# A four-layer graph network on one core: the third sort inside the first eight attention blocks, linear scores as table columns, operands in PSUM

## The chip, the cores and the metric

The kernel runs on one core of a Trainium2 chip. The time is device microseconds (us) of one execution. In the text, PE is TensorE (matmul), DVE is VectorE, ACT is ScalarE, POOL is GpSimd and SP is SyncE, whose queue only starts transfers here. SBUF is the on-chip memory of 128 partitions; PSUM is the smaller one that PE writes its sums into, which DVE and ACT can read and write too.

## The reference

3125 nodes with 64 features, 100000 edges sorted by destination, and four layers in a row, each on the normalised and rectified features, each added to its input. The layer that the change is about is the first:

```python
def _L0_gnn_ref(node_attr, edge_index, Wl, Wr, att, W1, b1, W2, b2):   # N = 3125, H = 4, DH = 16
    ngl = (node_attr @ Wl.T).reshape(N, H, DH)
    ngr = (node_attr @ Wr.T).reshape(N, H, DH)
    idx = jnp.concatenate([edge_index, edge_index[:, ::-1]], axis=0)      # every edge both ways
    src, dst = (idx[:, 0], idx[:, 1])
    gl = ngl[src]
    gr = ngr[dst]
    score = (att * jax.nn.leaky_relu(gl + gr, SLOPE)).sum(-1)             # SLOPE = 0.2
    m = jax.ops.segment_max(score, src, num_segments=N)
    ex = jnp.exp(score - m[src])
    denom = jax.ops.segment_sum(ex, src, num_segments=N)
    alpha = ex / (denom[src] + 1e-16)
    out = jax.ops.segment_sum(gr * alpha[:, :, None], src, num_segments=N)
    ...
```

The second layer (twice) and the third need sums of neighbours' rows over the 100000 edges, and the second a sum of the edges' own 64 attributes by destination. The fourth is an attention with eight heads over 31250 edges' worth of blocks of its own.

## The kernel before

The program is written by engine: one instruction stream each for SP, POOL, ACT, DVE and PE, ordered by hand and tied by semaphores. A `wait_ge` stops the engine that executes it, and all that stands behind it on that engine.

**Preparation (0 to 1324 us of the trace).** POOL scatters the edge attributes to records in DRAM (`scatter_recs`, L695: 98 groups of eight indirect DMAs of 128 rows each), then the 50 chunks of own rows (L715). Beside it DVE counts degrees with one-hot comparisons (`ones_of`, L1049: 336 bf16 comparisons of `iotab` with the edges' numbers, both in SBUF; PE multiplies them), and sorts three times with a bitonic network on 128 x 1024 numbers (`ordered`: 87 full comparison steps of a minimum and a maximum, L1203 and L1206; 66 partial ones of four instructions, L1212; 14 turns, in which PE transposes the block and DVE copies it back from PSUM, L1231 and L1233; 8 sign changes, L1220; 175 stages in all). The first two sorts order the edges by source and by destination for the attention; the third one (`KL`/`SBL` in the tile `oh`) orders them by cell of the adjacency matrix. Only the matrix units (below) need the third.

**The first attention (1324 to 3757 us).** 54 blocks of 128 partitions x 32 edge slots. For block g:

- POOL (`gather`, L738) waits until DVE has used the ring slot of block g - 4 (`taken0`, semaphore `av`), waits in `hold` (L688, a tiny addition on `pdum`) for the block's index list `jst`, and issues 32 indirect DMAs of 128 rows of 64 numbers from `tab[0]` into `G0`, a ring of four blocks. Before block 3 stands `gather_keys`: a hold for the third sort's result in DRAM, and nine indirect DMAs (L728) of windows of it.
- SP (`load_block`, L563) loads `jst` of block g + 3 once DVE has begun block g + 1 or so (`after(sp, S["aow"], b.g - 2)`), and stores the finished rows.
- DVE (`block0`): own rows (L1387), sum with the gathered rows (L1437, two halves of 1024), leaky slope (L1440, two), times `att` (L1442, two; `attb_ps` lies in PSUM), sum over 16 columns (L1444), then eleven short operations of the running maximum (L1395 to L1408). Then, beside the attention: matrix units (`matrix_ones`, L1414: one bf16 comparison of 2048 numbers of `iotab` with `SD`, both in SBUF, for each) and record groups (`rec_ones`, L1423). Then weights times rows (L1453, two; the weights are columns of `V0` in SBUF, which ACT fills), a sum over each row's four slots (L1460, from `V0` into `RS0`, both SBUF), and the carried scan (L1465 to L1467, `DX0` and `RS0` in SBUF).
- PE (`beside0`) multiplies each matrix unit (L1902) and each record group (L1910); ACT (`weights0`) takes the exponentials and casts and stores the units.

There are 272 units, `UAT`: five for each of the first 48 blocks, and `UL`: 6, 5, 5, 6, 5, 5 in the last six. Record groups: two a block, in the last six 4, 5, 4, 5, 4, 4. The first 48 blocks run as a loop of four, the last six are written out. Between the third sort and block 0, DVE and PE make the unit tables `SD` out of the nine windows (L1344 to L1355).

**After it** come the fix-up of rows cut by partitions, the neighbour sums of layers two and three, the second attention (same `gather` and L738, rows of 72 numbers) and the end.

## Time and profile before

| | us |
|---|---|
| median of 3 runs | 6147.66 |
| lowest, highest | 6140.43, 6149.96 |
| the profiled execution's own time | 6139.35 |
| its span | 6137.6 |

By stage, from the busy time of each engine in windows (us from the span's start):

| stage | length | DVE busy | POOL busy | PE busy |
|---|---|---|---|---|
| attribute scatter, degrees, two sorts, part of the third (109 to 1242) | 1133.0 | 946.6 | 901.0 | 385.6 |
| own rows (1242 to 1324) | 82.0 | 69.6 | 59.9 | 11.8 |
| blocks 0 to 2 are gathered (1324 to 1457) | 133.0 | 97.4 | 104.3 | 13.8 |
| key windows, unit tables (1457 to 1498) | 41.0 | 21.9 | 9.1 | 4.0 |
| blocks 3 to 53 (1498 to 3714) | 2216.0 | 1651.7 | 1725.2 | 695.4 |
| last block on DVE (3714 to 3757) | 43.0 | 35.3 | 0.7 | 19.1 |
| everything behind the first attention (3757 to 6137.6) | 2380.6 | | | |

### The profile page before, as it was taken

To read this page: it belongs to the slowest core of one execution; us is meant where nothing else is said; L and a number is where in the kernel's file an instruction comes from. 1 tells how busy PE (TensorE), PEld (TensorE's weight loads), DVE (VectorE), ACT (ScalarE), POOL (GpSimd) and SP (SyncE) were. 2 spreads that over 40 slices of the span, in tenths; PEclk is the share of its full clock that TensorE was granted. 3 is DMA by queue.
4 is the path that set the end of the run, shared out by engine and by line. 5 is a ranking of instruction groups with operands and counts; after the bars stand their busy time and mean duration, and the time that the engine had idled before them with its cause. 6 is when DMAs were issued, how large, how long until landed. Compare 5 with 4: busy or idle time off the path is not lost.

```text
span 6137.6 us, 56339 instructions
## 1 busy us (share of the span) xinstructions
PE 2661.9 (43%) x13332; PEld 1809.3 (29%) x13333; DVE 4092.7 (67%) x6865; ACT 1253.9 (20%) x4370; POOL 3783.2 (62%) x3760
## 2 busy tenths in 40 slices
PE   1785101011332322222222342677674577777746
PEld 0661101011322222222222242546453232332315
DVE  9778888886986776767676774232322576676655
ACT  0000000000111111111111110000000677777741
POOL 2777777776777777777777774000002777777730
PEclk6555555555555555555555555767685788888876
DMA  6221121211222222222222231435261222332230
GB/s 229 53 54 51 48 56 48 73 29 50 77 79 61 72 61 71 63 70 64 69 64 68 66 85 39 144 104 179 69 205 22 58 83 77 87 86 77 84 98 7
DMA packets 388365, 472.44 MB, mean 77 GB/s; under 512 B 212478, under 2 KB 248384, under 8 KB 381041
## 3 DMA queue, kind: packets, MB, share of 16 engines
q1 hardware_dynamic: 132624, 279.73, 13.8%
q0 software_dynamic: 114832, 129.82, 9.7%
q10 hardware_dynamic: 140752, 61.28, 3.5%
q14 instruction: 116, 0.94, 0.0%
q8 instruction: 41, 0.67, 0.0%
HBM read 291.34 MB, written 179.19 MB: 77 GB/s over the span
## 4 chain that ended last, share of the span: by engine, by line
POOL 58%; issue 21%; PE 9%; DMA 6%; DVE 5%; ACT 0%; POOLq 0%; DVEq 0%; ACTq 0%; SPq 0%
POOL arena L738 44%; POOL rec_dram L695 11%; PE acc L1959 4%; DMA oh<-mt_dram 2%; PE acc L1780 2%; DMA V<-in_edge_attr_dram 2%; DMA rec_dram<-V,rowst 1%; PE acc L1782 1%; PE acc L1943 1%; POOL own_dram L715 1%; POOL pdum L688 1%; POOL arena L765 1%; DVE arena L1579 1%; PE pt L1770 0%; POOL own_dram L769 0%
## 5 line engine op out<-in xcount | busy, mean ns | idle before, releaser
L738 POOL DMA_INDIRECT arena<-tab_dram,jst x2592 | 2685.8, 1036 | 778.3 <-issue 777.8
L695 POOL DMA_INDIRECT rec_dram<-V,rowst x784 | 866.1, 1105 | 229.9 <-issue 217.8
L688 POOL TENSOR_TENSOR pdum<-pdum 128x1 f32<-128x1 f32 x197 | 58.5, 297 | 1138.3 <-DVE arena L1607 864.6
L1902 PE MATMUL pw<-OHX 128*128 128x128 bf16 x1632 | 210.3, 310 | 1120.8 <-DVE OHX L1414 1120.8
L1902 PEld LDWEIGHTS pw<-OHX 128*128 128x128 bf16 x1632 | 156.9, 140 | 1172.3 <-DVE OHX L1414 859.7
L1910 PE MATMUL acc<-arena,oh 128*128 128x64 f32 x1952 | 427.1, 420 | 20.9 <-DVE oh L1423 20.7
L1910 PEld LDWEIGHTS acc<-arena,oh 128*128 128x128 f32 x1952 | 417.2, 330 | 34.9 <-issue 34.9
L900 ACT ACTIVATE arena<-arena,ew 128x64 f32<-128x64 f32 x1728 | 417.8, 333 | 33.3 <-PE acc L1983 33.3
L1437 DVE TENSOR_TENSOR arena<-arena,pt 128x1024 f32<-128x1024 f32 x108 | 131.8, 1221 | 431.7 <-DMA arena<-tab_dram,jst 429.4
L900 ACT ACTIVATE OHX<-arena,ew 128x64 f32<-128x64 f32 x1728 | 417.7, 333 | 2.5
L1983 PE MATMUL acc<-OHX,ident 128*128 128x512 f32 x432 | 253.7, 753 | 371.0 <-ACT OHX L900 371.0
L1855 PE MATMUL acc<-ident,oh 128*128 128x128 f32 x336 | 82.7, 427 | 752.3 <-DVE vdum L1224 752.3
L1212 DVE TENSOR_TENSOR oh<-oh 128x256 f32<-128x256 f32 x792 | 341.6, 431 | 37.8
L1855 PEld LDWEIGHTS acc<-ident,oh 128*128 128x128 f32 x336 | 65.9, 223 | 770.2 <-DVE vdum L1224 770.2
L855 ACT ACTIVATE arena<-dc 128x476 f32<-128x476 f32 x54 | 57.5, 1065 | 1143.3 <-DVE dc L1405 1143.3
L1959 PE MATMUL acc<-V,oh 128*128 x1440 | 234.7, 321 | 106.4 <-DVE arena L1579 86.5
L1579 DVE TENSOR_TENSOR arena<-arena,acc 128x192 f32 x360 | 127.6, 355 | 214.2 <-PE acc L1959 207.7
L1414 DVE TENSOR_TENSOR OHX<-iotab,OHX 128x2048 bf16<-128x2048 bf16 x204 | 249.7, 1224 | 28.0 <-DVE OHX L1414 15.6
L1983 PEld LDWEIGHTS acc<-OHX,ident 128*128 128x128 f32 x432 | 103.8, 248 | 520.1 <-issue 520.1
L825 ACT COPY V<-arena 128x8 f32 (+1 forms) x98 | 20.1, 205 | 1157.6 <-DMA rec_dram<-V,rowst 1080.5
L1902 PE MATMUL pw<-oh 128*128 128x128 bf16 x544 | 70.2, 310 | 386.2 <-DVE oh L1414 386.2
L1049 DVE TENSOR_TENSOR OHX<-iotab,arena 128x364 bf16<-128x364 bf16 x336 | 180.3, 536 | 64.5 <-DVE OHX L1049 17.9
(523 smaller groups left out, 6463.2 us busy)
## 6 DMA issues: line engine op xcount, KB each, us to landing
oh<-mt_dram SPq DMA_DIRECT2D x90, 512.0 KB, 3.6
arena<-tab_dram,jst POOLq DMA_INDIRECT x2592, 2.5
arena<-rec_dram SPq DMA_DIRECT2D x122, 288.0 KB, 3.6
mt_dram<-oh ACTq DMA_DIRECT2D x272, 128.0 KB, 1.7
oh<-mt_dram SPq DMA_DIRECT2D x75, 416.0 KB, 3.9
oh<-mt_dram SPq DMA_DIRECT2D x75, 384.0 KB, 4.0
rows_dram<-V SPq DMA_DIRECT2D x27, 1056.0 KB, 4.0
rows_dram<-arena SPq DMA_DIRECT2D x27, 1056.0 KB, 4.3
```

Source lines behind the costliest of these rows:

```text
L695: gp.indirect_dma_start(rec[:, :], bass.IndirectOffsetOnAxis(ap=rowst[:, q, k:k + 1], axis=0), recst[:, q, k, :], None).then_inc(S[f"scat{ ...
L738: gp.indirect_dma_start(hd.G[:, a.r, j, :], None, table[:, :], row_of(jst[:, a.r, j:j + 1])).then_inc(S[f"{x}g{a.r}"], 16)
L900: last = A.activation(V3r[vslot[f]][:, (k * H3 + h) * D:(k * H3 + h + 1) * D], G3[:, a.r, t, 0:D], ACT.Copy, scale=ew[:, a.q, t * H3 + h:t ...
L1049: V.tensor_tensor(paired(o[:, a:a + n]), iota_pairs(n, wide, EP), values[:, k, :].unsqueeze(2).to_broadcast([EP, n, wide // 2, 2]), ALU.is ...
L1212: V.tensor_tensor(o[r], a[r], b[r], op).then_inc(S["v"], 1)
L1414: V.tensor_tensor(paired(mones[c.slot].rearrange("p o t n -> p (o t) n")), iota_pairs(2 * GT, P), SD[:, bass.ds(c.u * (4 * GT), 4 * GT)].r ...
L1579: V.tensor_tensor(o, o, group_sum(g), ALU.add).then_inc(S["cadd"], 1)
L1855: last = nc.tensor.transpose(acc[:, (first + b) * P:(first + b + 1) * P], src[:, b * P:(b + 1) * P], ident[:])
L1902: last = nc.tensor.matmul(unit_bank(c.slot)[:, k // 2 * P:(k // 2 + 1) * P], mones[c.slot][:, 0, k, :], mones[c.slot][:, 1, k, :], start=k ...
L1910: last = nc.tensor.matmul(o, roh[:, c.q, k, :], RG[:, c.r, k, 0:D], start=False, stop=True, skip_group_check=True)
L1959: last = nc.tensor.matmul(group_sum(g), mring[:, slot, g * 4 + k, :], hsp[:, bass.ds(rows[g * 4 + k] * (3 * D), 3 * D)], start=k == 0, sto ...
L1983: last = nc.tensor.matmul(row_bank(2 * f + k // RK), ident[:], V3r[vslot[f]][:, k * 512:(k + 1) * 512], start=k % RK == 0, stop=k % RK == ...
```

## The change

Five things change together.

1. **Third sort in the blocks.** The list of 175 stages is cut: the first 104 run where the whole sort stood, the other 71 in eight parts inside DVE's blocks 0 to 7, behind the scores. The sort's two buffers move from `oh` to `OHX` (`SB3`), its transposes on PE from `acc` to `pw`. SP stores the keys behind block 7 (`store_keys`), POOL gathers the windows before block 12, and the unit tables are made in DVE's block 13 (`units_ready`), through `pw` in three parts.
2. **Units later.** Blocks 0 to 13 have no matrix units; blocks 14 to 53 have 272 x (g - 14) / 40 rounded down, so six or seven each. The blocks are written out on ACT, DVE and PE in place of the loop of four.
3. **Linear scores in the table.** leaky(z) is 0.2 z + 0.8 max(z, 0). The 0.2 part of the gathered row, times `att`, summed by head, is computed once for each node (`LIN`) and stored as four more columns of `tab[0]`, so a gathered row has 68 numbers. The own row's linear part is the same for all edges of a softmax and is left out. In the block one instruction does max and multiply.
4. **Weights, sums and compared numbers in PSUM.** ACT writes the weights a second time into PSUM (`wexp_ps`); the sums over slots go to `sums_ps` in two halves, so do the scans; `iotab` is copied to `pairs_ps`, which all one-hot comparisons read, those of the degree count too.
5. **Waits that go with it**: `tb` counts three tables, `ax` four activations a block, DVE waits for all weights' loads before `LIN`.

```diff
+SORTED_IN, SORT_FRONT = 8, 104
+UNITS_AT, KEYS_AT = SORTED_IN + 6, SORTED_IN + 4
...
-        KI = ohf_[:, 0:MT].bitcast(I)
-        KI2 = OHXf[:, 6400:6400 + MT // 2].bitcast(I)
+        SB3 = [OHXf[:, k * SWL:(k + 1) * SWL] for k in range(2)]
+        KI, KI2 = [OHXf[:, k * 1024:(k + 1) * 1024].bitcast(I) for k in range(2)]
...
-        iota_ps, attb_ps = pt[:, 512:512 + P], pt[:, 512 + P:512 + P + D]
+        pairs_ps, attb_ps = pt[:, 512:512 + P // 2], pt[:, 512 + P // 2:512 + P // 2 + D]
         own_ps = pt[:, 0:RB * D].rearrange("p (f d) -> p f d", d=D)
+        wexp_ps = pt[:, 0:TB * H0].rearrange("p (t h o) -> p t h o", h=H0, o=1)
+        half_x = (D + H0) // 2
+        sums_ps = [pt[:, k:k + half_x * RB] for k in (TB * H0, 1024 - half_x * RB)]
...
+        def unit_at(g):
+
+            return max(g - UNITS_AT, 0) * NU // (NB0 - UNITS_AT)
...
+        def sort_part(g):
+
+            rest = len(edge_sort) - SORT_FRONT
+            at_ = [0 if h < 0 else SORT_FRONT + rest * min(h, SORTED_IN) // SORTED_IN for h in (g, g + 1)]
+            return edge_sort[at_[0]:at_[1]]
...
-                quads(gp, n, rows)
+                if hd is heads0:
+                    quads(gp, n, rows, 0, KEYS_AT // 4)
+                    held[0] += KEYS_AT
+                    gather_keys()
+                    held[0] -= KEYS_AT
+                    quads(gp, n, rows, KEYS_AT // 4)
+                else:
+                    quads(gp, n, rows)
...
+                A.activation(wexp_ps, ew[:, a.q, 0:TB * H0].rearrange("p (t h o) -> p t h o", h=H0, o=1), ACT.Exp).then_inc(S["ax"], 1)
...
-                return iotab[0:parts, 0:wide].rearrange("p (n e) -> p n e", e=2).unsqueeze(1).to_broadcast([parts, tiles, wide // 2, 2])
+                return pairs_ps.bitcast(BF)[0:parts, 0:wide].rearrange("p (n e) -> p n e", e=2).unsqueeze(1).to_broadcast([parts, tiles, wide // 2, 2])
...
-            V.tensor_copy(GR, acc_n).then_inc(S["tsrc"], 1)
+            v.wait_ge(S["wts"], 16 * 29)
+            link(V.tensor_copy(GR, acc_n))
+            link(V.tensor_tensor(nbr_r[:], GR, attb[:].unsqueeze(1).to_broadcast([P, NC, D]), ALU.mult))
+            link(V.tensor_reduce(LIN, nbr_r[:].rearrange("p c (h e) -> p c h e", h=H0), AX, ALU.add))
+            V.tensor_scalar(LIN, LIN, SLOPE, None, ALU.mult).then_inc(S["tsrc"], 1)
...
+                    for hf in range(2):
+                        wv = work[:, hf * 1024:(hf + 1) * 1024].rearrange("p (t d) -> p t d", d=D)
+                        st(V.scalar_tensor_tensor(wv, wv, 0.0, attb_ps.unsqueeze(1).to_broadcast([P, TB // 2, D]), ALU.max, ALU.mult))
                     st(V.tensor_reduce(sc[:, 0:TB * H0], work.rearrange("p (x e) -> p x e", e=D // H0), AX, ALU.add))
+                    by_head = sc[:, 0:TB * H0].rearrange("p (t h) -> p t h", h=H0)
+                    st(V.tensor_tensor(by_head, by_head, Ga[:, :, D:D + H0], ALU.add))
                 scores(heads0, a, st, summed)
+                if a.g < SORTED_IN:
+                    sort_more(a)
+                if a.g == UNITS_AT - 1:
+                    units_ready()
...
+                for k, part in enumerate(sums_ps):
+                    ins = V.tensor_reduce(part.rearrange("p (x f) -> p f x", f=RB), V0[:, :, 2 * k:2 * k + 2].rearrange("p (f k) h e -> p f (h e) k", k=RK), AX, ALU.add)
```

**POOL, from the own rows to the first gathers**, before and then changed: `own_dram` is the own rows' scatter, `ps` two single gathers, `arena<-tab_dram,jst` a block of 32, `OHX<-keys_dram` the key windows, `pdum` the holds.

```order
L715 DMA own_dram<-arena,rst_u 61696x64 x50
L688 TENSOR_TENSOR pdum<-pdum 128x1 x2
L719 DMA ps<-tabl_dram,nfi 128x64 x2
...
L688 TENSOR_TENSOR pdum<-pdum 128x1
L738 DMA arena<-tab_dram,jst 128x64 x32
L688 TENSOR_TENSOR pdum<-pdum 128x1 x3
L728 DMA OHX<-keys_dram,arena 128x256 x8
L728 DMA OHX<-keys_dram,arena 64x256
L688 TENSOR_TENSOR pdum<-pdum 128x1
L738 DMA arena<-tab_dram,jst 128x64 x32
```

```order
L729 TENSOR_TENSOR pdum<-pdum 128x1
L779 DMA arena<-tab_dram,jst 128x68 x32
L385 REGISTER_ALU
L385 COMPARE_AND_BRANCH
L729 TENSOR_TENSOR pdum<-pdum 128x1 x3
L769 DMA OHX<-keys_dram,arena 128x256 x8
L769 DMA OHX<-keys_dram,arena 64x256
```

Before, the key windows stand behind the third block's gathers; now they stand behind the loop that ends with the twelfth, and a gathered row has 68 numbers.

**DVE, block 0 of the first attention from the gathered rows on**, before and then changed (`arena` holds the gathered rows, `work`, `DX0` and `RS0`; `pt` is PSUM; `OHX` and `oh` hold the one-hot tables; the eleven short operations of the maximum stand where the first row of "..." is).

```order
L1437 TENSOR_TENSOR arena<-arena,pt 128x1024 x2
L1440 SCALAR_TENSOR_TENSOR arena<-arena 128x1024 x2
L1442 TENSOR_TENSOR arena<-arena,pt 128x1024 x2
L1444 TENSOR_REDUCE sc<-arena 128x128
...
L1414 TENSOR_TENSOR OHX<-iotab,OHX 128x2048 x3
L1414 TENSOR_TENSOR oh<-iotab,OHX 128x2048
L1414 TENSOR_TENSOR OHX<-iotab,OHX 128x2048
L1423 TENSOR_TENSOR oh<-pt,arena 128x1024 x2
L1453 TENSOR_TENSOR V<-arena,V 128x64x16 x2
L1460 TENSOR_REDUCE arena<-V 128x8x68
L1465 TENSOR_TENSOR V<-V,dc 128x68
L1466 TENSOR_TENSOR arena<-arena,V 128x68
```

```order
L1495 TENSOR_TENSOR arena<-arena,pt 128x1024 x2
L1499 SCALAR_TENSOR_TENSOR arena<-arena,pt 128x1024 x2
L1500 TENSOR_REDUCE sc<-arena 128x128
L1502 TENSOR_TENSOR sc<-sc,arena 128x128
...
L1261 TENSOR_TENSOR OHX<-OHX 128x32x2x4 x4
...
L1483 TENSOR_TENSOR oh<-pt,arena 128x1024 x2
L1515 TENSOR_TENSOR V<-arena,pt 128x64x16 x2
L1523 TENSOR_REDUCE pt<-V 128x8x34 x2
L1531 TENSOR_TENSOR V<-V,dc 128x68
L1534 TENSOR_TENSOR pt<-pt,V 128x34 x2
L1537 SCALAR_TENSOR_TENSOR V<-arena,pt 128x272 x2
```

The five comparisons of block 0 have become eight stages of the sort (from L1261 on); multiply, reduce and scan have one operand in `pt` where both lay in SBUF.

## Rows read from the trace of the kernel before

**Rows 1.** The page, chain that ended last, by line: share of the span.

```profile
POOL arena L738 44%; POOL rec_dram L695 11%; PE acc L1959 4%; DMA oh<-mt_dram 2%; PE acc L1780 2%; DMA V<-in_edge_attr_dram 2%; DMA rec_dram<-V,rowst 1%; PE acc L1782 1%; PE acc L1943 1%; POOL own_dram L715 1%; POOL pdum L688 1%; POOL arena L765 1%; DVE arena L1579 1%; PE pt L1770 0%; POOL own_dram L769 0%
```

**Rows 2.** POOL's timeline: start us, duration us, what, [idle before <-releaser].

```profile
1324.04 1.08 POOL L738 DMA_INDIRECT arena<-tab_dram,jst  x1 [0.16 <-issue]
...
1456.87 0.74 POOL L688 TENSOR_TENSOR pdum<-pdum 128x1 f32<-128x1 f32 x3
...
1497.68 0.19 POOL L688 TENSOR_TENSOR pdum<-pdum 128x1 f32<-128x1 f32 x1 [28.89 <-DMA jst<-meta_dram]
...
3712.89 0.94 POOL L738 DMA_INDIRECT arena<-tab_dram,jst  x1 [0.30 <-issue]
```

**Rows 3.** POOL's groups, 1498 to 3715 us: count, busy us, mean ns, idle.

```profile
L738 POOL DMA_INDIRECT arena<-tab_dram,jst x1632 | 1714.2, 1050 | 489.9 <-issue 489.6
```

**Rows 4.** Timeline of POOL and of DVE, around 1506 us.

```profile
1506.47 1.92 POOL L738 DMA_INDIRECT arena<-tab_dram,jst  x1 [0.30 <-issue]
...
1506.35 3.74 DVE L1414 TENSOR_TENSOR OHX<-iotab,OHX 128x2048 bf16<-128x2048 bf16 x3
```

**Rows 5.** Timeline of POOL and of DVE, 1562 to 1568 us.

```profile
1563.64 0.94 POOL L738 DMA_INDIRECT arena<-tab_dram,jst  x1 [0.30 <-issue]
...
1566.13 1.17 POOL L738 DMA_INDIRECT arena<-tab_dram,jst  x1 [0.30 <-issue]
...
1562.75 2.48 DVE L1437 TENSOR_TENSOR arena<-arena,pt 128x1024 f32<-128x1024 f32 x2
1565.26 2.48 DVE L1440 SCALAR_TENSOR_TENSOR arena<-arena 128x1024 f32<-128x1024 f32 x2
```

**Rows 6.** Timeline of POOL and of DVE, while the third sort runs.

```profile
1395.76 1.15 POOL L738 DMA_INDIRECT arena<-tab_dram,jst  x1 [0.30 <-issue]
...
1395.39 0.69 DVE L1203 TENSOR_TENSOR oh<-oh 128x512 f32<-128x512 f32 x1
```

**Rows 7.** POOL's groups, 180 to 440 us, then 440 to 447; DVE's by form.

```profile
L695 POOL DMA_INDIRECT rec_dram<-V,rowst x180 | 198.7, 1104 | 54.2 <-issue 51.2 <-DMA V<-in_edge_attr_dram 3.0
...
L695 POOL DMA_INDIRECT rec_dram<-V,rowst x6 | 5.8, 965 | 1.8 <-issue 1.8
...
L1049 DVE TENSOR_TENSOR OHX<-iotab,arena 128x896 bf16<-128x896 bf16 x224 | 140.7, 628 | 32.7 <-DVE OHX L1049 9.4
```

**Rows 8.** DVE's groups by form, 1490 to 3757 us.

```profile
L1414 DVE TENSOR_TENSOR OHX<-iotab,OHX 128x2048 bf16<-128x2048 bf16 x204 | 249.7, 1224 | 28.0 <-DVE OHX L1414 15.6 <-DVE oh L1414 6.9 <-PE pw L1902 4.5
L1460 DVE TENSOR_REDUCE arena<-V 128x544 f32<-128x2176 f32 x54 | 209.2, 3874 | 1.9
...
L1440 DVE SCALAR_TENSOR_TENSOR arena<-arena 128x1024 f32<-128x1024 f32 x108 | 132.7, 1229 | 3.7
...
L1437 DVE TENSOR_TENSOR arena<-arena,pt 128x1024 f32<-128x1024 f32 x108 | 131.8, 1221 | 431.7 <-DMA arena<-tab_dram,jst 429.4
...
L1467 DVE TENSOR_TENSOR_SCAN V<-arena 128x544 f32<-128x544 f32 x54 | 69.8, 1292 | 1.9
...
L1395 DVE TENSOR_TENSOR sc<-sc,jst 128x128 f32<-128x128 f32 x54 | 17.2, 318 | 1.9
```

**Rows 9.** DVE's timeline: blocks 21, 49 and 53 begin.

```profile
2327.11 2.48 DVE L1437 TENSOR_TENSOR arena<-arena,pt 128x1024 f32<-128x1024 f32 x2 [10.85 <-DMA arena<-tab_dram,jst]
...
3548.47 2.48 DVE L1437 TENSOR_TENSOR arena<-arena,pt 128x1024 f32<-128x1024 f32 x2 [5.00 <-DMA arena<-tab_dram,jst]
...
3716.24 2.47 DVE L1437 TENSOR_TENSOR arena<-arena,pt 128x1024 f32<-128x1024 f32 x2 [1.79 <-DMA arena<-tab_dram,jst]
```

**Rows 10.** DVE's groups, whole span: a 2048-number cast out of PSUM.

```profile
L1349 DVE CAST oh<-acc 128x2048 int32<-128x2048 f32 x1 | 2.3, 2293 | 4.1 <-PE pt L1888 4.1
```

**Rows 11.** Line L738, both attentions: duration ns min/median/max, first and last start us.

```profile
L738 POOL DMA_INDIRECT arena<-tab_dram,jst x2592: 940/944/2000, 1324.0 to 5870.2; - x200
```

**Rows 12.** DVE's timeline: begin and end of the third sort.

```profile
1136.07 86.55 DVE L1212 TENSOR_TENSOR oh<-oh 128x256 f32<-128x256 f32 x180
...
1436.84 0.06 DVE L1340 MEMSET vdum<- 1x1 f32 x1
```

More of the change, by code:

```diff
@@ L387, in quads, with spans @@
                     body(Group(n // 4, t))
-        def spans(eng, n, ahead, step):
+        def spans(eng, n, ahead, step, cut=4, between=None):
             def at(i, t):
@@ L395, in spans @@
                 at(0, t)
-            with eng.Fori(1, whole) as i:
-                for t in range(4):
-                    at(i, t)
+            for i, e in ((1, cut // 4), (cut // 4, whole)):
+                if i == cut // 4 and between:
+                    between()
+                if i + 1 == e:
+                    for t in range(4):
+                        at(i, t)
+                elif i < e:
+                    with eng.Fori(i, e) as turn:
+                        for t in range(4):
+                            at(turn, t)
             for t in range(4 * whole, n):
@@ L531, in _ @@
             table(1, GL, tabl)
-            table(2, GR, tab[0])
+            table(2, GR, tab[0][:, 0:D])
+            table(2, LIN, tab[0][:, D:D + H0])
             sp.wait_ge(S["pre"], 3)
```

269 lines of the change are left out of this document (146 added, 123 removed).

## The prediction, made before the changed kernel ran

> **What bounds the kernel now.** I read the chain that ended last first: 44% of the span is one line, POOL's row gathers of the two attentions [rows 1]. So the question for each stage is whether POOL ever waits. In POOL's timeline over the first attention the reader is to see that it begins at 1324.04, gathers blocks 0 to 2 until 1456.87, does the nine key windows, stands 28.89 us, and from 1497.68 to 3713.83 never stands again [rows 2]. The releaser named is block 3's index list, but SP could not issue it before DVE began block 0, and DVE began late since it still had to finish the third sort and the unit tables. DVE in turn waits 10.85 us before block 21, of a period of 2370.81 - 2327.11 = 43.7 us (the next start is the next block's): it has 32.9 us of work in a block [rows 9]. The first attention is POOL's.
>
> Then I asked what one gather costs. The median is 0.944 us with a minimum of 0.940, for rows of 64 and of 72 numbers together [rows 11], but the mean of the 1632 gathers of blocks 3 to 53 is 1.050, with 0.30 between two [rows 3]. The difference, 1632 x 0.106 = 173 us, is what DVE does to POOL. Seen one by one: a gather that begins 0.12 us after a comparison with both inputs in SBUF takes 1.92, and ends 0.8 us behind the end of that comparison, the first of three in 3.74 us [rows 4]. One that begins while DVE adds an SBUF and a PSUM operand takes 0.94; one that begins 0.4 us before the first of two slope operations (both inputs `work`) ends takes 1.17, which is that end plus 0.8 again [rows 5]. Reading all gathers of the stretch against DVE's rows that way, those that begin outside an operation with two SBUF inputs never exceed 0.96. While the sort runs, gathers keep step with two of its 0.69 us operations and take 1.15, so 1.45 a piece with the gap instead of 1.244 [rows 6].
>
> **A rule against this.** The Trainium skill, "SBUF — State Buffer", section "Who interferes with whom", tells of a probe in which `tensor_copy` held up GpSimd's DMAs and `tensor_tensor` did not. Rows 4 to 6 differ: here it does, and the rows decide. By the rule the PSUM operands would give POOL nothing, which is rival 2.
>
> **The change, part by part**, in the trace's own time (span 6137.6, execution 6139.35).
>
> *Degree count.* Its comparisons read `pairs_ps` instead of `iotab`. In 180 to 440 us, 180 scatters take 1.104 us; when the comparisons have ended, six take 0.965 [rows 7]. POOL scatters without a pause, so all behind moves forward: 180 x 0.139 = **-25**. From below 0, if only half is port and DMA staging takes the rest. `LIN` adds some 6 us to DVE (three passes over 1600 numbers), which DVE has: it ends the second sort long before POOL needs it. The wait for the weights' loads is moved to where they have long landed.
>
> *The idle time before block 3.* The whole sort took 1436.84 - 1136.07 = 300.8 us [rows 12]. Its 66 partial steps cost 86.55/45 = 1.92 each, the 87 full ones 2 x 0.69 + 0.07 = 1.45, so 14 turns and 8 sign changes share 48. The front, 52 partial, 40 full, seven turns, five signs, is 100 + 58 + 24 = 182 us and ends near 1136 + 6 + 182 = 1324; the rest is 119, or 14.9 a block. DVE is then ready before block 0's rows have landed (1299 + 43), SP's queue reaches the index list of block 3 at once, and the wait of 28.89 is gone: **-29**. The key windows (12 us) only move, and the unit tables, which fitted into that wait, go into DVE's block 13, which has no units. What queues behind that wait on DVE is only its own block: POOL is a ring of four ahead.
>
> *Blocks.* POOL now needs 132.8 for blocks 0 to 2 and 2216.2 for the other 51 [rows 2], together 2349.0. A clean block is 32 x (0.944 + 0.30) + 0.5 for hold and wait = 40.3. Comparisons, slope, weights times rows and scan lose their second SBUF input; what keeps two is short (0.2 to 0.37 us each, as L1395 [rows 8]), say 0.1 a block: 40.4. In the first eight blocks 14.9 us of sort cover ten gathers that lose 0.2 each: 42.4. While the front still runs beside block 0, 3.3 more. Sum 8 x 42.4 + 46 x 40.4 + 3.3 = 2200.9: **-148**.
>
> A row of 68 numbers lies between widths that share one median [rows 11], so it costs nothing.
>
> *What hides DVE's work.* Two of 1.229 go, one of 0.32 comes, the split sums and scans add some 0.3: -1.9 [rows 8]. In the first eight blocks also five comparisons of 1.26 go and 14.9 of sort come: 32.9 - 1.9 - 6.3 + 14.9 = 39.6, under POOL's 42.4. Blocks 14 to 47 have 6.8 units: 32.9 - 1.9 + 2.3 = 33.3, under 40.4. Not seen before are sums and scans into and out of PSUM. The two sums cost at least 2.4, by 1024 numbers in 1.221, at most 2 x 3.87; I take 4.0, near the one they replace. The scans lie between 1.3 and 2.6; I take 1.4. With both at their worst the block is 38.3, still covered in the middle. ACT's additional exponential of 128 numbers is hidden by the sort, the units or the two record groups.
>
> *The end.* The last six blocks have 26 record groups that alternate with PE, and DVE needs about 40.6, 42.8, 39.7, 44.1 and 39.4 for blocks 48 to 52 (ends of [rows 9]: only 1.79 us is left before block 53). That was hidden by 43.4. With -1.9, and one or two more units each, they are 40.0, 42.2, 40.3, 43.5 and 40.0 against 40.4: DVE falls 4.4 behind, and block 53 is 0.6 longer: **+5**, or +35 with sums and scans at their worst.
>
> Sum: -25 - 29 - 148 + 5 = -197, so 5942 for such an execution. The median of the runs was 8.3 above the profiled one: **5951 us**.
>
> **Rivals.**
> 1. *PSUM takes the double rate away.* The comparison of 2048 bf16 numbers takes 1.224 [rows 8], twice the rate of f32, where 2048 out of PSUM take 2.293 [rows 10]. No row shows bf16 out of PSUM. If it goes at the single rate, the 336 of the degree count take 224 x 0.47 + 112 x 0.19 = 126 us more, DVE begins block 0 near 1450, POOL has ended block 2 at 1432 and waits 23, with 5 more under the sort; the 41 units of the last six blocks add 41 x 1.07 = 44. Together 5951 + 72 = **6023**. The Trainium skill, "VectorE: DVE Perf Modes", has this rule in "The perf-mode tier table" (`tensor_tensor` with any PSUM operand 1x), while its section "Why PSUM operands drop a tier" leaves the packed 2x mode open. Against it: f32 with one PSUM operand costs what two SBUF ones cost (1.221 and 1.229 [rows 8]).
> 2. *POOL gets nothing from PSUM operands.* Then only the wait goes, and the sort slows eight blocks: 8 x 44.8 + 46 x 43.4 = 2355, +6, with -29 and +1: 6117 + 8 = **6126**. Against it stand rows 4 and 5.
> 3. *DVE becomes the bound: slower than before.* From 7.1 us a block above my 33.3 it sets the pace of blocks 14 to 53, and from some 12 it eats all. Comparisons at the single rate (7.3), sums at 7.7 (+3.7) and scans at 2.6 (+1.2) would do it: 40 x (45.5 - 40.4) = 204, with 28 at the start and 12 more at the end **6195**. It needs every PSUM operand dear at once, which the f32 rows speak against.
>
> **How the numbers follow.** My forecast has 0.78, rival 1 0.11, rival 2 0.08, rival 3 0.03. The forecast's own range is 5920 (DVE's sums at the low bound, blocks at 40.3, more scatters freed) to 6000 (no gain in the degree count, or the worst end). With rival 1 it reaches to 6040; rivals 2 and 3 are left out, and the edges of the others. Within 0.2% is about 12 us, what a measurement of this kernel can tell from no change: faster 0.96, same 0.01, slower 0.03.
>
> **What would show it.** In the changed profile: scatters of 180 to 440 us at 0.97; block 3's hold with no wait; the group of the first attention's gathers at a mean near 0.95, about 1.0 in blocks 0 to 7; DVE's comparison at 1.22 (2.29 is rival 1); a wait of some 7 us on DVE for rows in the middle blocks and none in the last six; POOL's last gather near 3512, DVE's last block near 3557. A mean of 1.05 would be rival 2. Wrong would be also a new wait of POOL on `av` (DVE more than three blocks late), or gathers of 68 numbers at more than 0.95 on their own.

## The result, and the profile of the changed kernel

The changed kernel takes **5926.45 us** (median of four runs, 5924.3 to 5928.3) against 6147.95 before; the ratio is 0.9642, with a 95% interval of 0.9625 to 0.9658. The forecast was 5951, in a range of 5920 to 6040. The profiled execution of the changed kernel took 5926.62 with a span of 5923.7, so 213.9 us of span are gone, where the sum said 197.

In the page of the changed kernel the row gathers of the two attentions, now on line L779, still head the chain that ended last, with 35% of the span in place of 44% [rows 1]:

```profile
POOL arena L779 35%; POOL rec_dram L736 11%; PE acc L2039 4%; DMA oh<-mt_dram 2%; DVE OHX L1473 2%; PE acc L1854 2%; PE acc L1856 1%; PE acc L2023 1%; POOL own_dram L756 1%; DMA V<-in_edge_attr_dram 1%; DMA rec_dram<-V,rowst 1%; PE acc L1990 1%; DVE oh L1483 1%; DVE arena L1495 1%; DVE V L1515 1%
```

POOL's groups of the changed kernel, first from 180 to 440 us (the degree count's stretch, as [rows 7]), then from 1296 to 3489 us (all 54 blocks of the first attention, as [rows 3]). Columns: count | busy us, mean ns | idle before, releaser:

```profile
L736 POOL DMA_INDIRECT rec_dram<-V,rowst x200 | 195.1, 976 | 60.1 <-issue 60.1
...
L779 POOL DMA_INDIRECT arena<-tab_dram,jst x1728 | 1650.7, 955 | 518.5 <-issue 515.5 <-DVE V L1515 3.0
```

The first row: 200 scatters fit where 180 did, 0.976 us each instead of 1.104. The second: a gather takes 0.955 on the mean instead of 1.050, and nearly all idle time is the 0.30 between two. POOL's and DVE's timelines of the changed kernel show the ends of the stages (start, duration, what, [idle before <-releaser]), as [rows 2, 9]:

```profile
1296.12 0.96 POOL L779 DMA_INDIRECT arena<-tab_dram,jst  x1 [0.35 <-issue]
...
1420.43 0.21 POOL L729 TENSOR_TENSOR pdum<-pdum 128x1 f32<-128x1 f32 x1
...
3487.79 0.94 POOL L779 DMA_INDIRECT arena<-tab_dram,jst  x1 [0.30 <-issue]
...
3532.95 1.47 DVE L1537 TENSOR_TENSOR_SCAN V<-arena,pt 128x272 f32<-128x272 f32 x2
```

The gathers begin at 1296.12 instead of 1324.04. The hold of block 3 (the addition on `pdum` at 1420.43) waits for nothing; before it waited 28.89. The last gather ends at 3488.73 instead of 3713.83, and DVE's last scan at 3534.42, 45.7 behind it; before these were 39.1 (3752.90 behind 3713.83). DVE's groups by form, 1640 to 3536 us, answer to [rows 8]; below them, the scan that ended before's last block:

```profile
L1473 DVE TENSOR_TENSOR OHX<-pt,OHX 128x2048 bf16<-128x2048 bf16 x204 | 249.5, 1223 | 5.9
L1523 DVE TENSOR_REDUCE pt<-V 128x272 f32<-128x1088 f32 x94 | 191.4, 2037 | 3.2
...
L1499 DVE SCALAR_TENSOR_TENSOR arena<-arena,pt 128x1024 f32<-128x1024 f32 x92 | 112.3, 1220 | 3.1
...
L1537 DVE TENSOR_TENSOR_SCAN V<-arena,pt 128x272 f32<-128x272 f32 x94 | 67.7, 720 | 3.2
```

```profile
3751.61 1.29 DVE L1467 TENSOR_TENSOR_SCAN V<-arena 128x544 f32<-128x544 f32 x1
```

A bf16 comparison with one input in PSUM still takes 1.223, so rival 1 is out. The Trainium skill, "VectorE: DVE Perf Modes", has it at the single rate in the section "The perf-mode tier table" and leaves the packed rate open in "Why PSUM operands drop a tier"; this row shows the double rate. The two sums take 4.07 (4.0 assumed), the two scans 1.44 (1.4).

**The books.** From the start of the span to the first gather: -27.9. The idle time before block 3: -28.9. The blocks: before 2349.0 (the prediction's own count), now 3488.73 - 1296.12 = 2192.6, less 12.0 for the key windows in block 12, is 2180.6: -168.4. From POOL's last gather to DVE's last scan: +6.6. What follows: +4.6, nearly all in the neighbour sums, which the change doesn't touch: POOL waits there for DVE 864.6 us in the profile of before, 869.3 in the changed kernel's and 866.3 to 871.9 in those of parts 1, 3 and 4 below, whatever was changed, so before's profile had a short one. With 0.1 for the key windows the sum is -213.9.

A gather is called caught below when it lasts clearly longer than its own 0.944 us, and its excess is what it lasts over 0.944. Added up over the 1728 gathers of the first attention, the excess was 186 us before and is 20 now, nearly all of it in blocks 0 to 8 and in block 14.

### The profile page after: what moved, and what is told of

Its sections match the earlier page's. It is cut to its first block, busy times and chain, and to the rows that moved or that the text cites. A ratio compares the mean times of both kernels' runs of the same rounds, so it can differ in the third digit from the quotient of the medians.

```text
span 5923.7 us, 53534 instructions
## 1 busy us (share of the span) xinstructions
PE 2662.1 (45%) x13332; PEld 1808.8 (31%) x13333; DVE 4000.1 (68%) x6981; ACT 1264.8 (21%) x4424; POOL 3582.9 (60%) x3760
## 4 chain that ended last, share of the span: by engine, by line
POOL 50%; issue 20%; DVE 13%; PE 11%; DMA 5%; ACT 0%; POOLq 0%; DVEq 0%; SPq 0%; ACTq 0%
POOL arena L779 35%; POOL rec_dram L736 11%; PE acc L2039 4%; DMA oh<-mt_dram 2%; DVE OHX L1473 2%; PE acc L1854 2%; PE acc L1856 1%; PE acc L2023 1%; POOL own_dram L756 1%; DMA V<-in_edge_attr_dram 1%; DMA rec_dram<-V,rowst 1%; PE acc L1990 1%; DVE oh L1483 1%; DVE arena L1495 1%; DVE V L1515 1%
## 5 line engine op out<-in xcount | busy, mean ns | idle before, releaser
L779 POOL DMA_INDIRECT arena<-tab_dram,jst x2592 | 2519.3, 972 | 778.1 <-issue 775.0
L736 POOL DMA_INDIRECT rec_dram<-V,rowst x784 | 837.5, 1068 | 231.6 <-issue 224.0
L729 POOL TENSOR_TENSOR pdum<-pdum 128x1 f32<-128x1 f32 x197 | 53.1, 270 | 1122.5 <-DVE arena L1681 869.3
L1929 PE MATMUL acc<-ident,oh 128*128 128x128 f32 x224 | 55.1, 428 | 487.7 <-DVE vdum L1273 487.7
L1473 DVE TENSOR_TENSOR OHX<-pt,OHX 128x2048 bf16<-128x2048 bf16 x204 | 249.5, 1223 | 5.9
L1261 DVE TENSOR_TENSOR oh<-oh 128x256 f32<-128x256 f32 x528 | 227.6, 431 | 24.6
L1523 DVE TENSOR_REDUCE pt<-V 128x272 f32<-128x1088 f32 x108 | 219.9, 2037 | 3.7
L1096 DVE TENSOR_TENSOR OHX<-pt,arena 128x364 bf16<-128x364 bf16 x336 | 178.6, 532 | 64.2 <-PE pt L1905 18.5
L2023 PE MATMUL acc<-V,oh 128*128 128x192 bf16 x1875 | 174.3, 251 | 88.7 <-DMA oh<-mt_dram 52.4
```

What stands on the lines that cost most here:

```text
L736: gp.indirect_dma_start(rec[:, :], bass.IndirectOffsetOnAxis(ap=rowst[:, q, k:k + 1], axis=0), recst[:, q, k, :], None).then_inc(S[f"scat{ ...
L779: gp.indirect_dma_start(hd.G[:, a.r, j, :], None, table[:, :], row_of(jst[:, a.r, j:j + 1])).then_inc(S[f"{x}g{a.r}"], 16)
L1261: V.tensor_tensor(o[r], a[r], b[r], op).then_inc(S["v"], 1)
L1473: V.tensor_tensor(paired(mones[c.slot].rearrange("p o t n -> p (o t) n")), iota_pairs(2 * GT, P), SD[:, bass.ds(c.u * (4 * GT), 4 * GT)].r ...
L1523: ins = V.tensor_reduce(part.rearrange("p (x f) -> p f x", f=RB), V0[:, :, 2 * k:2 * k + 2].rearrange("p (f k) h e -> p f (h e) k", k=RK), ...
L2023: last = nc.tensor.matmul(group_sum(a.t // 2), mring[:, a.t % 4, k, :], hsp[:, j * (3 * D):(j + 1) * (3 * D)], start=j == 0, stop=j == NC ...
```

## Experiments

Each kernel's runs stand beside runs of the kernel before on the same chip. Differences from the changed kernel are against its median of 5926.45. With the chip of part 2 left out, before's medians were 6142.1 to 6148.0, so a difference between kernels of two chips is good to some 6 us.

**1. One part undone at a time.** Four kernels on one chip (before: 6142.1 there).

The first, `u1_compare_sbuf`:

```diff
                 V.tensor_tensor(paired(mones[c.slot].rearrange("p o t n -> p (o t) n")),
-                                iota_pairs(2 * GT, P),
+                                iota_sbuf(2 * GT, P),
...
-                V.tensor_tensor(roh[:, c.q], pairs_ps.bitcast(BF).unsqueeze(1).to_broadcast([P, GT, P]),
+                V.tensor_tensor(roh[:, c.q], iotab[:].unsqueeze(1).to_broadcast([P, GT, P]),
```

> The changed kernel with one part undone: the comparisons of the first attention's matrix units and record groups read their row of numbers from SBUF again. In the kernel before, the excess over 0.944 us of the gathers that began in such a comparison adds up to 78 us over 51 blocks, 1.5 a block. Theory A (each comparison costs what it cost there): 40 blocks with units and 54 with record groups give +60 to +80 us, gathers' mean about 1.00. Theory B (a train of comparisons brings the gathers into step with it, 1.26 us each instead of 1.244, so that only the first of a train costs much): +12 to +20. Rival 2 of the prediction (the operand's place doesn't matter to POOL): within 0.2% of the changed kernel.

Measured: 5962.0 us, **+35.6**, between the two theories and nearer to B. The edit undoes more than the change did: in the kernel before only the matrix units' comparisons read SBUF alone; those of the record groups read PSUM already (`oh<-pt,arena`, L1423). Here, and in `u4_blocks_sbuf` and `u6_all_sbuf` below, these read SBUF too, and the gathers that they catch have an excess of 12 to 13 us, some 7 of it in blocks 49 to 53. So what the change moved is worth some 23 of the 35.6. The next, `u2_degree_sbuf`, undoes the degree count's operand alone:

```diff
-                    V.tensor_tensor(paired(o[:, a:a + n]), iota_pairs(n, wide, EP),
+                    V.tensor_tensor(paired(o[:, a:a + n]), iota_sbuf(n, wide, EP),
```

> The changed kernel with the degree count's comparisons reading from SBUF again, nothing else. My theory: the scatters of 180 to 440 us go back from 0.976 to about 1.10 us each and all behind them starts 28 us later (1324 instead of 1296 for the first gather): +28 in the total. If something else had moved the start forward, no change.

Measured: 5956.8, **+30.4**. POOL's group of 180 to 440 us is back where before's was [rows 7], or a little above (1.125 us each, 1.104 before):

```profile
L736 POOL DMA_INDIRECT rec_dram<-V,rowst x179 | 201.4, 1125 | 52.2 <-issue 50.4 <-DMA V<-in_edge_attr_dram 1.8
```

`u3_sort_front` does the whole third sort ahead of the blocks:

```diff
-SORTED_IN, SORT_FRONT = 8, 104
+SORTED_IN, SORT_FRONT = 8, 175
```

> The changed kernel with all 175 stages of the third sort ahead of block 0, none in the first eight blocks. DVE then begins block 0 near 1443 us instead of 1340. My theory: the gathers of blocks 0 to 2 keep step with the sort (1.45 us each with the gap, 46.4 a block instead of 41.6: +14), POOL stands about 15 us before block 3, and blocks 3 to 8 run at 40.1 instead of 41.7 (-10): +20 us. If carrying the sort into the blocks had brought nothing: no change.

Measured: 5944.1, **+17.7**. In POOL's timeline the gathers of blocks 0 to 2 keep step with the sort, and the hold of block 3 waits again:

```profile
1343.47 1.13 POOL L779 DMA_INDIRECT arena<-tab_dram,jst  x1 [0.30 <-issue]
...
1429.95 1.14 POOL L779 DMA_INDIRECT arena<-tab_dram,jst  x1 [0.30 <-issue]
...
1447.92 0.20 POOL L729 TENSOR_TENSOR pdum<-pdum 128x1 f32<-128x1 f32 x1 [16.82 <-DMA jst<-meta_dram]
```

`u4_blocks_sbuf` has the edit of the first, and:

```diff
-            link(V.tensor_scalar(attb_ps, attb[:], 1.0 - SLOPE, None, ALU.mult))
+            link(V.tensor_scalar(attb_sb[:], attb[:], 1.0 - SLOPE, None, ALU.mult))
...
-                        st(V.scalar_tensor_tensor(wv, wv, 0.0, attb_ps.unsqueeze(1).to_broadcast([P, TB // 2, D]), ALU.max, ALU.mult))
+                        st(V.scalar_tensor_tensor(wv, wv, 0.0, attb_sb[:].unsqueeze(1).to_broadcast([P, TB // 2, D]), ALU.max, ALU.mult))
...
-                                          wexp_ps[:, ts].to_broadcast([P, TB // 2, H0, D // H0]), ALU.mult)
+                                          V0[:, ts, :, D // H0:].to_broadcast([P, TB // 2, H0, D // H0]), ALU.mult)
```

> As the first, and also the weights and the attention vector of the slope operation come from SBUF again; only the sums, the scans and the degree count keep PSUM. By theory A the shares in the kernel before add up: 78 for the comparisons, 34 for the slope operation, 14 for the weights, 1.05 as the gathers' mean: +110 to +125. By theory B the second and third add little: +18 to +40.

Measured: 5970.1, **+43.6**: with the weights and the attention vector it is 8 us more than with the comparisons alone. Theory A (110 to 125) is refuted, and theory B (18 to 40) is passed by 4. The three parts undone give 30.4 + 17.7 + 43.6 = 92 of the 221.5 us between the two medians, and some 12 of them are the record groups', so more than half of the gain doesn't come back when they are undone.

**2. Four more kernels, of which only one told something.** On the chip that ran them every kernel was some 1800 us longer (before 7952.2), and in the profiles the engines stood at moments for 10 to 20 us, DVE in the degree count for up to 113 us, in front of an instruction, released by what the profile calls "remote". POOL waited there for index lists that depend on DVE's progress, 848 us in `b1_compare_psum`, where the kernel before has 36, so DVE set the pace, and the four are not compared with the others.

`b1_compare_psum`, made from the kernel before:

```diff
-                V.tensor_tensor(paired(mones[c.slot].rearrange("p o t n -> p (o t) n")), iota_pairs(2 * GT, P),
+                V.tensor_tensor(paired(mones[c.slot].rearrange("p o t n -> p (o t) n")),
+                                pairs_ps.bitcast(BF).rearrange("p (n e) -> p n e", e=2).unsqueeze(1).to_broadcast([P, 2 * GT, P // 2, 2]),
```

> The kernel before with one part of the change alone: the comparisons of the matrix units in the first attention read their row of numbers from PSUM. In the trace of before such a block has one gather of 1.92 us and four of 1.07 to 1.09 under the five comparisons, 1.5 us over 0.944 together. Theory A (what is undone is gained): 51 x 1.5 = -77 us. Theory B (a gather caught by one operation shifts all behind it, so others are caught instead): -25 to -60. If the place of the operand doesn't matter: no change.

Measured: 8003.4 against 7952.2, ratio 1.0068 (1.0046 to 1.0091): inconclusive, and not repeated.

`b3_straight`, made from the kernel before:

```diff
-            quads(eng, NB0, body, 0, LAST // 4)
-            for t in range(LAST, NB0):
+            for t in range(NB0):
                 body(Group(t // 4, t % 4))
```

> The kernel before with another part alone: the blocks of the first attention written out on PE, ACT and DVE instead of a loop over four, no operand moved. In before DVE stands 0.15 us between two comparisons of the loop and their pitch is 1.38 us; in the changed kernel without the loop it is 1.26, next to the 1.24 of the gathers. Theory B: the four later gathers under the comparisons take 0.95 instead of 1.08, 47 blocks x 0.5 = -25 us. Rival: the loop only costs DVE, which has slack, so no change.

Measured: 7970.0, ratio 1.0024 (1.0010 to 1.0038): inconclusive, repeated below.

`u5_all_sbuf` has the edits of `u4_blocks_sbuf`, and:

```diff
-        sums_ps = [pt[:, k:k + half_x * RB] for k in (TB * H0, 1024 - half_x * RB)]
+        sums_ps = [arena[:, 12800:12800 + half_x * RB], arena2[:, 6112:6112 + half_x * RB]]
```

> The changed kernel with comparisons, weights, attention vector, sums and scans of the first attention all in SBUF again (u4_blocks_sbuf plus sums and scans; the degree count keeps PSUM). The excess of gathers that began in the scan of before was 46 us over 51 blocks. Theory A: +48 over u4_blocks_sbuf. Theory B (two scans of 0.70 us, less to be caught by, and the phase is as it falls): +10 to +35 over it, so 5980 to 6005.

Measured: 7909.9, ratio 0.9937 (0.9913 to 0.9962): inconclusive, repeated below.

`p1_kinds` is the kernel of part 3 with one operation of each kind and another list of kinds.

> The changed kernel with one more DVE operation at the start of each of blocks 16 to 47, where DVE waits for rows anyway (its output is overwritten, nothing is left out): four blocks for each kind. Kinds in order: tensor_tensor f32 with both inputs in SBUF; the same with one in PSUM; tensor_reduce f32; copy f32; tensor_scalar f32; copy bf16; tensor_tensor bf16 with both in SBUF; tensor_scalar bf16, all from SBUF. Theory: only the first and the seventh make a gather that starts in them last until their end plus 0.8 us (up to 3.1 us for one of 2.3); under all others gathers take 0.94. Rival: what matters is an operation's speed, so the fast copies hold gathers too and the first, at 1 number a cycle, doesn't. The total: within 0.3% of the changed kernel.

Measured: 7865.0. The total says nothing, but a gather can be read against the operation in which it begins on any chip. Under the first kind, gathers that began 0.84 and 1.25 us into 2.3 took 2.26 and 1.89; under the second and third all took 0.94. But a gather that began 0.33 into the fifth kind, an f32 `tensor_scalar` with one input, took 1.71, which is its end plus 0.8, and the two copies and the bf16 `tensor_scalar` caught gathers too (1.38 to 1.60). My theory of two SBUF inputs was too narrow.

**3. Which operations hold a gather.**

```diff
+            def probe(kind):
...
+                times, op = ((2, lambda: V.tensor_tensor(f32, f32, att_s, ALU.mult)),
+                             (2, lambda: V.tensor_tensor(f32, f32, att_p, ALU.mult)),
+                             (2, lambda: V.tensor_copy(f32, att_p)),
+                             (3, lambda: V.tensor_copy(f32, att_s)),
+                             (3, lambda: V.tensor_scalar(f32, f32, 0.5, None, ALU.mult)),
+                             (3, lambda: V.tensor_copy(b16, row)),
+                             (2, lambda: V.tensor_reduce(sc[:, 0:TB * H0], work.rearrange("p (x e) -> p x e", e=D // H0), AX, ALU.max)),
+                             (3, lambda: V.tensor_scalar(b16, row, 0.5, None, ALU.mult)))[kind]
...
+                if H == H0 and 16 <= a.g < 48:
+                    probe((a.g - 16) // 4)
                 v.wait_ge(S[f"{x}g{a.r}"], (a.turn + 1) * 16 * TB)
```

> p1_kinds again with operations in pairs or threes, so that more gathers begin in each kind. p1_kinds showed that my theory of two SBUF inputs is too narrow: a tensor_scalar of 2048 f32 in 1.23 us held a gather as well. New theory: what holds POOL is an operation with two inputs in SBUF at any rate, or one with one SBUF input at the fast rate (2048 f32 or 4096 bf16 in 1.23 us); one with a PSUM input, and a reduction, never do. Kinds in order: tensor_tensor f32 both SBUF; tensor_tensor f32 one PSUM; copy f32 out of PSUM; copy f32 SBUF; tensor_scalar f32 SBUF; copy bf16 SBUF; tensor_reduce f32; tensor_scalar bf16 SBUF. Expected: gathers begun in the first, fourth, fifth, sixth and eighth end 0.8 us behind the operation in which they began; in the second, third and seventh all take 0.94. Total within 0.5% of the changed kernel.

Measured: 5964.8 (before 6143.8 beside it). POOL's gathers of four blocks for each kind, in the order of the expectation (the stretches 1966 to 2135, 2136 to 2295, 2296 to 2455, 2456 to 2623, 2625 to 2792, 2793 to 2960, 2962 to 3120 and 3122 to 3289 us):

```profile
L779 POOL DMA_INDIRECT arena<-tab_dram,jst x128 | 130.3, 1018 | 38.4 <-issue 37.5 <-DVE V L1535 0.9
...
L779 POOL DMA_INDIRECT arena<-tab_dram,jst x128 | 120.8, 944 | 38.4 <-issue 38.1 <-DVE V L1535 0.3
...
L779 POOL DMA_INDIRECT arena<-tab_dram,jst x128 | 120.8, 944 | 38.4 <-issue 37.8 <-DVE V L1535 0.6
...
L779 POOL DMA_INDIRECT arena<-tab_dram,jst x128 | 129.1, 1009 | 38.4 <-issue 37.8 <-DVE V L1535 0.6
...
L779 POOL DMA_INDIRECT arena<-tab_dram,jst x127 | 128.1, 1008 | 38.2 <-issue 37.6 <-DVE V L1535 0.6
...
L779 POOL DMA_INDIRECT arena<-tab_dram,jst x128 | 129.4, 1011 | 38.4 <-issue 38.4
...
L779 POOL DMA_INDIRECT arena<-tab_dram,jst x128 | 120.9, 944 | 38.4 <-issue 38.4
...
L779 POOL DMA_INDIRECT arena<-tab_dram,jst x128 | 129.3, 1010 | 38.4 <-issue 38.4
```

Five kinds raise the mean, as expected: both inputs in SBUF, and every one-input operation from SBUF at the fast rate. Three don't: one input in PSUM, a copy out of PSUM, a reduction. The fifth kind in the timelines of DVE and POOL:

```profile
2658.15 3.75 DVE L1440 TENSOR_SCALAR arena<-arena 128x2048 f32<-128x2048 f32 x3
...
2657.76 1.73 POOL L779 DMA_INDIRECT arena<-tab_dram,jst  x1 [0.30 <-issue]
2659.80 2.22 POOL L779 DMA_INDIRECT arena<-tab_dram,jst  x1 [0.30 <-issue]
```

The first of these gathers began 0.39 us ahead of the three operations and was held all the same, to 0.11 behind the end of the first (1.23 us); the second to 0.12 behind the end of the third. That I had not expected: where another fast operation follows at once, the gather does not end 0.8 us behind the operation in which it began, as I had written, but 0.12 behind the next. It still ends 0.82 behind where none follows: in the fifth kind's fourth block one gather began in the last of the three and took 1.66. In the four fast kinds every gather that began up to 0.48 ahead was caught, and those that began 0.77 ahead, and in `p1_kinds` 0.53 ahead, took their 0.94. Under the two-input operation those that began 0.37 to 0.39 ahead took 0.94. The Trainium skill, "SBUF — State Buffer", section "Who interferes with whom", says that copies and `tensor_scalar` at the two-port rates block GpSimd, that reductions don't, and, as an inference, that `tensor_tensor` doesn't hold descriptor generation. The rows agree with the first two and contradict the third.

**4. The rest of the gain, and a version that goes on.** Three kernels on one chip (before: 6143.6).

> The same kernel as b3_straight, on a chip on which the kernel before runs at its usual time: the kernel before with the blocks of the first attention written out, no operand moved. Theory B: the gaps of 0.15 us between two comparisons go, gathers keep step with them at 0.95 instead of 1.08: -25 us. Rival: the loop costs DVE alone, which has slack: no change.

The edit is that of b3_straight. Measured: 6107.6, **-35.9** (ratio 0.9940, 0.9924 to 0.9957), more than the 25 expected. The loop cost POOL, not DVE alone: 33 of it are less excess in the first attention (186 to 153 us), by the profiles. DVE's and POOL's timelines in one block of the middle:

```profile
2530.55 2.48 DVE L1439 SCALAR_TENSOR_TENSOR arena<-arena 128x1024 f32<-128x1024 f32 x2
...
2540.28 1.22 DVE L1413 TENSOR_TENSOR OHX<-iotab,OHX 128x2048 bf16<-128x2048 bf16 x1
2541.53 1.22 DVE L1413 TENSOR_TENSOR oh<-iotab,OHX 128x2048 bf16<-128x2048 bf16 x1
2542.78 3.74 DVE L1413 TENSOR_TENSOR OHX<-iotab,OHX 128x2048 bf16<-128x2048 bf16 x3
...
2556.15 1.29 DVE L1466 TENSOR_TENSOR_SCAN V<-arena 128x544 f32<-128x544 f32 x1
...
2530.71 1.88 POOL L737 DMA_INDIRECT arena<-tab_dram,jst  x1 [0.30 <-issue]
...
2540.39 1.91 POOL L737 DMA_INDIRECT arena<-tab_dram,jst  x1 [0.30 <-issue]
2542.61 0.95 POOL L737 DMA_INDIRECT arena<-tab_dram,jst  x1 [0.30 <-issue]
2543.87 0.95 POOL L737 DMA_INDIRECT arena<-tab_dram,jst  x1 [0.30 <-issue]
...
2556.43 1.77 POOL L737 DMA_INDIRECT arena<-tab_dram,jst  x1 [0.30 <-issue]
```

The comparisons follow at 1.26 us. The first gather among them begins 0.11 behind the start of the first comparison and is caught until 0.8 behind its end. Each later one begins 0.13 to 0.14 before the end of a comparison, and 0.82 behind that end is also where its own 0.95 ends: it runs at 0.95 + 0.31 = 1.26, in step with them, so a train of operations costs once. In the loop of before DVE stood 0.15 between two comparisons, their pitch was 1.38, and in most blocks each later gather among them took 1.07 to 1.09, waiting for the same 0.82 behind an end that came 0.13 later. What is left in this block is one catch each in the slope operation, the first comparison and the scan: 0.94 + 0.97 + 0.83 = 2.7.

> The same kernel as u5_all_sbuf, on a chip on which the kernel before runs at its usual time: comparisons, weights, attention vector, sums and scans of the first attention in SBUF again. Theory A (each scan costs what it cost in before, 46 us together): 6018. Theory B (what an operation costs depends on where the gathers fall against it, so the sum of the shares of before is not to be had back): 5980 to 6005.

The edit is that of u5_all_sbuf. Measured: 5971.2, **+44.7**, which is `u4_blocks_sbuf` again (5970.1): sums and scans in PSUM are worth about 1 us, no more than the two chips differ by, and even theory B's 10 was too much. The same kinds of operands stand in SBUF as in `b4_straight`, and those of the record groups as well, yet a block of the middle loses half as much:

```profile
2557.51 2.48 DVE L1504 SCALAR_TENSOR_TENSOR arena<-arena,attb_sb 128x1024 f32<-128x1024 f32 x2
...
2565.07 1.22 DVE L1478 TENSOR_TENSOR OHX<-iotab,OHX 128x2048 bf16<-128x2048 bf16 x1
...
2582.62 1.48 DVE L1542 TENSOR_TENSOR_SCAN V<-arena 128x272 f32<-128x272 f32 x2
...
2557.63 1.92 POOL L780 DMA_INDIRECT arena<-tab_dram,jst  x1 [0.30 <-issue]
...
2564.87 1.11 POOL L780 DMA_INDIRECT arena<-tab_dram,jst  x1 [0.30 <-issue]
2566.28 0.95 POOL L780 DMA_INDIRECT arena<-tab_dram,jst  x1 [0.30 <-issue]
...
2583.78 1.08 POOL L780 DMA_INDIRECT arena<-tab_dram,jst  x1 [0.30 <-issue]
```

The slope operation still catches a gather (1.92). The gather at the comparisons began in the short subtraction ahead of them and lost 0.17 instead of 0.97; the next began 0.04 ahead of a comparison and took 0.95. The one at the scan lost 0.14 instead of 0.83. In both kernels DVE starts a block when the rows of a gather land, so its operations stand at nearly fixed offsets against the gathers; here, with one wide multiplication gone, one short addition in and the scan halved, the offsets are better.

How sharp an offset is, the slope operation of this one kernel shows. Of the 31 blocks 17 to 47, 20 are like the one above and take 41.4 us; in the other 11 the slope operation catches none, and they take 40.2. In `b4_straight` most take 42.9. Such a block of the other sort, DVE and POOL:

```profile
2517.44 2.48 DVE L1504 SCALAR_TENSOR_TENSOR arena<-arena,attb_sb 128x1024 f32<-128x1024 f32 x2
...
2517.40 0.95 POOL L780 DMA_INDIRECT arena<-tab_dram,jst  x1 [0.30 <-issue]
```

Operation, operands and kernel are the same in all 31. In the 20 a gather began 0.047 to 0.120 us behind the start of the first of the two operations and took 1.92 to 2.00; in the 11 it began between 0.051 ahead and 0.038 behind and took 0.94 or 0.95, and where it began behind, DVE's operation lasted 1.27 to 1.30 instead of 1.22. Some 0.01 us of offset decides which of the two engines waits, and whether POOL loses a whole microsecond.

The whole first attention by the profiles: the excess is 153 us in `b4_straight` and 74 in `u6_all_sbuf`. Between the two some 35 us went in the scans, 46 in the matrix units' comparisons with the subtraction ahead of them, 7 in the slope operations and 4 in the weights' multiplication, and 12 came with the record groups.

> A version that may beat both kernels: the changed kernel, and in the second attention the exponentials of weights and of state factors go to PSUM, where DVE's wide multiplications read them (rows of sums rotate over seven PSUM banks instead of eight to make room, blocks written out on PE and DVE), and the units of the last six blocks of the first attention move into blocks 14 to 47. My theory: the 864 gathers of the second attention, mean 1.005 us in the changed kernel, go to 0.945, -52 us, with DVE idle about 10 of 42 us there and ACT about 9; DVE no longer ends the first attention late, -5: 5870. Rival: with seven banks PE waits for DVE's additions, DVE for PE, and DVE or ACT sets the pace of the second attention: 5900 to 5930.

The main parts of its edit; the second attention's wide multiplications read `ew_ps` and `dc_ps`, and its blocks are written out on PE and DVE:

```diff
-            return acc[:, f * 512:(f + 1) * 512] if f < 4 else (accw, pu, pt[:, 0:512], pt[:, 512:1024])[f - 4]
+            f = f % 7
+            return acc[:, f * 512:(f + 1) * 512] if f < 4 else (accw, pu, pt[:, 0:512])[f - 4]
+        ew_ps = pt[:, 512:512 + TB * H3]
+        dc_ps = pt[:, 768:768 + 2 * RB * H3].rearrange("p (q f h) -> p q f h", q=2, f=RB)
...
-                A.activation(dc[:, a.q], dc[:, a.q], ACT.Exp).then_inc(S["dx"], 1)
+                A.activation(dc_ps[:, a.q], dc[:, a.q], ACT.Exp).then_inc(S["dx"], 1)
+                A.activation(ew_ps, ew[:, a.q], ACT.Exp).then_inc(S["dx"], 1)
...
-            return max(g - UNITS_AT, 0) * NU // (NB0 - UNITS_AT)
+            return min(max(g - UNITS_AT, 0) * NU // (LAST - UNITS_AT), NU)
```

Measured: **5864.6** (5858.7 to 5871.4), ratio to before 0.9542 (0.9526 to 0.9558): better than both kernels. POOL's group over the second attention of the changed kernel, then of this one, and this one's last scan of the first attention:

```profile
L779 POOL DMA_INDIRECT arena<-tab_dram,jst x864 | 868.5, 1005 | 259.6 <-issue 259.6
```

```profile
L783 POOL DMA_INDIRECT arena<-tab_dram,jst x864 | 823.1, 953 | 259.5 <-issue 257.7 <-ACT arena L951 1.5 <-DVE OHX L1722 0.3
...
3524.27 1.48 DVE L1542 TENSOR_TENSOR_SCAN V<-arena,pt 128x272 f32<-128x272 f32 x2
```

The second attention gives 45 of the 52 us expected, and PE, ACT and DVE stay under it with seven banks. The blocks are also written out there, which alone gave something in the first attention, but the timelines tell the two apart. In the changed kernel 56 of the 221 gathers that begin in a wide multiplication are caught, with 44 of the 53 us of excess; in this one none of the 207 that do takes more than 0.95, and the excess left is 7.5. The scan ends 30.4 us behind POOL's last gather (3495.36) instead of 45.7: the units taken out of the last six blocks give 15 there, more than the 5 expected. In this profile the first gather stood 7 us later than in the changed kernel's. That builds up over the scatters under the first two sorts (0.2 us late at the 251st, 8.0 at the last); why they caught more there stays open.

## Why the prediction was right, point by point

*The bound.* POOL stays the bound of the first attention, and none of the rivals came. The double rate held (rival 1), gathers of blocks 15 to 47 take 0.944 (rival 2), DVE waited 7.1 us in the middle blocks where 7 was forecast (rival 3).

*Degree count, -25.* -27.9 in the profile, and 30.4 when undone. The price of one scatter was right (0.976 for 0.965); since they are faster, 200 fall into the stretch in place of 180, and each gains.

*The idle time, -29.* The 28.89 before block 3 are gone. Undoing the carried sort costs 17.7 and not 29, near the 20 expected there: in the first eight blocks the sort takes part of it back.

*Blocks, -148.* This term was mis-sized: it is -168.4. Blocks 9 to 53 (less the key windows and the unit tables) repeat in 40.04 us where I had 40.4: the short two-input operations, priced at 0.1, catch next to nothing; hold and wait lengthen the step from one block's last gather to the next block's first by 0.07 and not by 0.5; against that a gather with its gap takes 1.249 and not 1.244, 0.16 a block. 46 x 0.36 = 17. Blocks 0 to 7 take 333.3 together where 8 x 42.4 + 3.3 = 342.5 was forecast: six to eleven gathers are held in each, where ten were assumed. Block 8, gathered while DVE still sorts in its block 7, took 41.5. Block 14 took 3.9 more than its neighbours, under the unit tables' subtractions and conversions, for which the prediction charged POOL nothing; `p3_kinds` shows that fast one-input operations are not free either. The term was taken from what a block costs with no gather caught, and that held. The reason given for it, that the excess goes because the operands move to PSUM, holds only in part: undoing all of them in the blocks costs 44.7, some 12 of it by the record groups' comparisons, which read PSUM before too, and the written-out blocks, which the prediction didn't price, are worth 35.9 alone. With the degree count and the sort that is 30.4 + 17.7 + 32.7 + 35.9 = 117 of 221.5. A sum from the clean block comes out right whichever part of the change frees the gathers, so that the split was wrong didn't show in it. The other 100 or so are in what the experiments didn't take apart: the multiplication that went, the halved scans, the moved units. The rows of `b4_straight` and `u6_all_sbuf` show most of them as gathers caught for 0.1 to 0.2 instead of 0.8 to 1.0, or not at all. That the offset decides is shown for the slope operation by the 31 blocks above; that better offsets are what the three parts brought is read from the rows and was not tried by moving one operation alone.

*The end, +5.* +6.6 to DVE's last scan; DVE begins blocks 49 to 53 without a wait, where the forecast had all of the last six. Sums and scans cost what was taken.

*From the sum to the median.* I added 8.3 us, by which before's profiled run lay under its median. The changed kernel's profiled run lies on its median. That is a third of the miss of 24.5 us; the blocks are 20 and the degree count 3, and +4.6 in the neighbour sums and 1.6 at the end go the other way. That the next median would again lie 8.3 above its profiled run had nothing behind it but one case.

## What to carry to other kernels

Where GpSimd issues indirect DMAs all the time, read their durations one by one against what DVE runs at that moment: mean minus minimum, times count, is the prize, and one input of DVE's wide operations placed in PSUM collects part or all of it, as the second attention showed with 45 of 53 us. Don't add up what single operations cost in the trace of before: a train of operations without gaps costs one catch, gaps of 0.15 us between them cost each later gather 0.13, and a few hundredths of a microsecond of offset decide whether an operation costs 1 us or none. A loop on an engine with slack can cost the engine that has none. The same reading shows what this change leaves: behind the degree count 532 scatters still take 1.097 us on the mean, most of them caught by the sorts' comparisons with both inputs in SBUF, some 70 to 80 us in all.
